# Four merged expert slots per unit, placed irregularly among the score batches of an attention and mixture-of-experts layer

## The reference, cut to what matters

```
q, k, v = xn @ Wq.T, xn @ Wk.T, xn @ Wv.T              # 16 heads of 16
attn    = softmax(q k^T / 16) v                        # 4096 keys and 4096 queries a head
h_e     = silu((xn @ w1_e + b1_e) * (xn @ w3_e + b3_e))    # hidden width 352
experts = shared expert + the two best of 8 experts, weighted by softmax(xn @ gate.T)
```

## Time and profile before

| what | us |
|---|---|
| median of three runs | 2263.67 (2261.61 to 2264.11) |
| the profiled execution, its own time | 2250.58 |
| span of the profiled execution | 2248.8 |
| TensorE busy | 2207.4 (98%) |
| TensorE weight loads | 962.0 (43%) |
| ScalarE busy | 2025.7 (90%) |
| VectorE busy | 793.5 (35%) |
| GpSimd busy | 238.6 (11%) |
| mean granted TensorE clock | 0.996 |

### The profile page before, as it was taken

One profiled execution on the slowest core, in us unless ns is written; L12 is line 12 of the kernel. 1 busy time (PEld: TensorE's weight loads), 2 busy tenths in 40 slices (PEclk: granted clock), 3 DMA queues, 4 the chain that ended last, 5 costly groups with the idle time before them and its releaser, 6 DMA issues.

```text
span 2248.8 us, 38025 instructions
## 1 busy us (share of the span) xinstructions
PE 2207.4 (98%) x15618; PEld 962.0 (43%) x15618; DVE 793.5 (35%) x1514; ACT 2025.7 (90%) x2209; POOL 238.6 (11%) x242
## 2 busy tenths in 40 slices
PE   7989999999999999999999999999999999999998
PEld 3622344444444444444444444444444444444322
DVE  6312133333333333343333333333343333333132
ACT  4579999999999999999999999999999999999997
POOL 1000242223221000000000000000000000000172
PEclk9989999999999999999999999999999999999999
DMA  6661333132232223213132222213213222221142
GB/s 228 214 247 59 81 99 91 59 100 85 75 90 71 64 50 77 74 52 83 41 79 68 73 62 67 74 48 81 73 48 82 62 60 68 79 62 40 49 136 79
DMA packets 219374, 187.28 MB, mean 83 GB/s; under 512 B 107815, under 2 KB 190334, under 8 KB 218942
## 3 DMA queue, kind: packets, MB, share of 16 engines
q1 hardware_dynamic: 207374, 149.41, 23.7%
q0 software_dynamic: 11824, 35.40, 4.8%
HBM read 130.21 MB, written 54.53 MB: 82 GB/s over the span
## 4 chain that ended last, share of the span: by engine, by line
PE 93%; ACT 6%; issue 1%; DVE 0%; DMA 0%; DVEq 0%
PE PS L627 40%; PE PS L614 29%; PE PS L639 13%; PE PS L650 6%; ACT probs L800 6%; PE PS L522 3%; PE PS L559 1%; PE PS L511 0%; PE PS L532 0%; DMA resid<-in_x 0%; DVE ln_t L907 0%; DVE o_t L1093 0%; DVE stats L902 0%; DVE probs L926 0%; ACT hid L791 0%
## 5 line engine op out<-in xcount | busy, mean ns | idle before, releaser
L800 ACT ACTIVATE probs<-PS 128x1024 f32<-128x1024 f32 x2048 | 1935.7, 1083 | 147.7 <-PE PS L614 139.9
L627 PE MATMUL PS<-probs,v_head 128*32 128x512 f32 x8192 | 999.1, 600 | 1.2 <-ACT probs L800 0.8
L614 PE MATMUL PS<-q_ring,k_stack 50*128 50x512 f32 x4096 | 779.0, 454 | 15.5 <-issue 9.7
L614 PEld LDWEIGHTS PS<-q_ring,k_stack 50*128 50x128 f32 x4096 | 319.4, 185 | 599.5 <-ACT probs L800 525.9
L627 PEld LDWEIGHTS PS<-probs,v_head 128*32 128x32 f32 x8192 | 207.2, 109 | 458.9 <-issue 455.5
L1124 DVE SCALAR_TENSOR_TENSOR prod<-PS,bias_sb,gate_in 128x256 f32<-128x256 f32 x165 | 79.6, 482 | 514.7 <-PE PS L639 514.7
L639 PE MATMUL PS<-x_hi,w_hi 128*128 128x256 f32 (+1 forms) x660 | 217.6, 330 | 0.0
L639 PE MATMUL PS<-x_lo,w_hi 128*128 128x256 f32 (+1 forms) x660 | 185.6, 281 | 0.0
L639 PE MATMUL PS<-x_hi,w_lo 128*128 128x256 f32 (+1 forms) x660 | 185.4, 281 | 0.0
L1118 DVE TENSOR_SCALAR gate_in<-PS,bias_sb 128x256 f32<-128x256 f32 x165 | 79.7, 483 | 297.3 <-PE PS L639 297.3
L854 POOL DMA_DIRECT2D slot_y<-y_sb x39 | 27.9, 716 | 1387.3 <-DVE y_sb L1187 1387.3
(11 more groups left out here) (128 smaller groups left out, 1042.2 us busy)
## 6 DMA issues: line engine op xcount, KB each, us to landing
w_raw<-in_w SPq DMA_DIRECT2D x110, 352.0 KB
k_stack<-qk_parts SPq DMA_DIRECT2D x120, 128.0 KB
w_raw<-in_w SPq DMA_DIRECT2D x55, 256.0 KB
q_ring<-qk_parts SPq DMA_DIRECT2D x384, 32.0 KB
slot_x<-part_a SPq DMA_DIRECT2D x39, 256.0 KB, 2.3
slot_in<-slot_x SPq DMA_DIRECT2D x156, 64.0 KB, 2.4
slot_y<-y_sb POOLq DMA_DIRECT2D x39, 256.0 KB, 2.5
k_stack<-qk_parts SPq DMA_DIRECT2D x136, 64.0 KB
```

The source lines that it names most:

```text
L614: last = pe.matmul(bank(2 * score_buffer(turn, g) + r), k_stack[rows, kt * P:(kt + 1) * P], q_ring[rows, sweep, i * QC:(i + 1) * QC], star ...
L627: last = pe.matmul(bank(O_BANK)[VW * j:VW * (j + 1), :], v_head[:, kt, :], probs[:, slot, (j % 2) * QC:(j % 2 + 1) * QC], start=(kt == 0), ...
L800: nc.scalar.activation(probs[:, prob_slot(g), :], bank(2 * score_buffer(h, g), 2), ACT.Exp, scale=ENERGY_SCALE).then_inc(s_exp, 1)
```

## The change

TensorE gets another order within a unit, and three places on the other engines follow it. The eight slots become four: `up_both(u, j)` issues both halves of an up pair without a wait between them (twelve matmuls), and the two `down` calls of a unit stand directly behind each other (18 matmuls). One semaphore count for a pair replaces the two counts (`s_ab`: 3 a unit instead of 6). The score groups come in batches of two or three, the value tiles always in pairs. The number of score groups, value tiles and expert matmuls is the same. Waits for `s_exp` are now made from a running count: a value tile waits by itself where no score group before it has waited for as much.

```
-                last.then_inc(s_ab, 1)
+                return last
...
+            def up_both(u, j):
+                if u >= UNITS:
+                    return
+                if j == 0 and u == 0:
+                    pe.wait_ge(s_prc, 1)
+                if j == 0 and u > 0:
+                    pe.wait_ge(s_prod, 3 * u)
+                if j == 0:
                     pe.wait_ge(s_w13, u + 1)
                     pe.wait_ge(s_xboth, u + 1)
-                    up(u, 0, 0)
-                if i == 1 and u < UNITS:
-                    pe.wait_ge(s_gin, 3 * u + 1)
-                    up(u, 0, 1)
...
+                if j == 1 or (j == 2 and u == 0):
+                    pe.wait_ge(s_prod, 3 * u + j)
+                if j == 2 and u > 0:
+                    pe.wait_ge(s_yc, u)
+                up(u, j, 0)
+                up(u, j, 1).then_inc(s_ab, 1)
+
+            def down_tile(u, t):
+                if u < 0:
+                    return
+                if t == 0:
+                    if u + 1 < UNITS:
+                        pe.wait_ge(s_prod, 3 * u + 5)
+                    pe.wait_ge(s_w2, u + 1)
+                    pe.wait_ge(s_hlo, u + 1)
+                down(u, t)
+
+            issued = [0, 0, 0]
+
+            def next_scores(count):
+                for n in range(issued[0], issued[0] + count):
+                    if n >= SB:
+                        pe.wait_ge(s_exp, n - SB + 1)
+                        issued[2] = max(issued[2], n - SB + 1)
+                    if n < H * GH:
+                        scores(n // GH, n // GH, n % GH)
+                issued[0] += count
+
+            def next_values(count):
+                for m in range(issued[1], issued[1] + count):
+                    if issued[2] < 2 * m + 2:
+                        pe.wait_ge(s_exp, 2 * m + 2)
+                        issued[2] = 2 * m + 2
+                    values(m // GS, m // NT % 2, m % NT)
+                issued[1] += count
...
             def mixed_head(h):
...
+                for u in range((h - 1) * PER_HEAD, h * PER_HEAD):
+                    next_scores(3)
+                    up_both(u, 0)
+                    next_scores(2)
+                    next_values(2)
+                    next_scores(3)
+                    next_values(2)
+                    next_scores(3)
+                    next_values(2)
+                    next_scores(2)
+                    up_both(u, 1)
+                    next_scores(3)
+                    next_values(2)
+                    next_scores(3)
+                    next_values(2)
+                    next_scores(3)
+                    down_tile(u - 1, 0)
+                    down_tile(u - 1, 1)
+                    next_scores(3)
+                    next_values(2)
+                    next_scores(3)
+                    next_values(2)
+                    next_scores(2)
+                    up_both(u, 2)
+                    next_scores(2)
+                    next_values(2)
...
             def gate(u, j):
-                dve.wait_ge(s_ab, 6 * u + 2 * j + 1)
+                dve.wait_ge(s_ab, 3 * u + j + 1)
...
             def product(u, j):
                 dve.wait_ge(s_gin, 3 * u + j + 1)
-                dve.wait_ge(s_ab, 6 * u + 2 * j + 2)
...
             def tokens_hi(u):
-                dve.wait_ge(s_ab, 6 * u)
+                dve.wait_ge(s_ab, 3 * u)
...
                     if u:
                         hidden(u - 1)
-                    if real:
-                        gate(u, 1)
-                    if u:
                         hidden_hi(u - 1)
                         hidden_lo(u - 1)
                     if real:
+                        gate(u, 1)
                         product(u, 1)
```

More of the change, by code:

```diff
@@ L53 @@
 PER_HEAD = 4
-UNIT_STEPS = GS // PER_HEAD
+UNIT_GROUPS = GH // PER_HEAD
 TANH_LAG = 3
@@ L703, in plain_head @@
+            def plain_head(h):
                 for k in range(1, GS + 1):
-                    step_scores(h, k, last)
-                    if first and k == 20:
+                    next_scores(2)
+                    if h == 0 and k == 20:
                         pe.wait_ge(s_mask, 1)
@@ L710, in plain_head @@
                         pe.matmul(bank(F_BANK)[:, NT * E:2 * NT * E], ones_sb[:, :], cm, start=True, stop=True).then_inc(s_pre, 1)
-                    values(h, (k - 1) // NT, (k - 1) % NT)
+                    next_values(1)
             def mixed_head(h):
[L715 to L727, removed]
+                for u in range((h - 1) * PER_HEAD, h * PER_HEAD):
[22 more added lines that the diff above has]
+                    up_both(u, 2)
+                    next_scores(2)
+                    next_values(2)
+            next_scores(SB)
+            plain_head(0)
             for h in range(1, H - 1):
                 mixed_head(h)
-            plain_head(H - 1, last=True)
+            plain_head(H - 1)
         @block.scalar
@@ L802, in _ @@
                     done = (h - 1) * GH + g - TANH_LAG
-                    if done > 0 and done % (2 * UNIT_STEPS) == 0 and done // (2 * UNIT_STEPS) <= UNITS:
-                        tanh(done // (2 * UNIT_STEPS) - 1)
+                    if done > 0 and done % UNIT_GROUPS == 0 and done // UNIT_GROUPS <= UNITS:
+                        tanh(done // UNIT_GROUPS - 1)
         @block.gpsimd
```

## The result

The changed kernel takes 2243.47 us (median of four runs, 2241.7 to 2246.07) against 2263.84 us. The ratio is 0.9913 with a 95% interval of 0.9896 to 0.993: 0.9% faster. The forecast was 2239.7 us. The profiled execution took 2246.07 us, its span is 2244.3 us.

What follows compares the result with a forecast made beforehand. TensorE was taken to bound heads 1 to 14. Merged slots (0.76 us) and score batches (0.80) less added waits gained 0.43 us a unit; 54 units plus 1 us took 2263.67 to 2239.7 us, range 2222 to 2262.

Steps and rivals of the forecast that it cites:

- The unit: One period of TensorE's expert-stage order in heads 1 to 14: from 33.49 to 33.06 us, a gain of 0.43 us.
- the join: Between a merged slot's halves: matmuls follow at 0.12 us without edges, saving 0.76 us a unit over four merges.
- three late third scores: Last group of a second batch of three, three times a unit: 0.14 us wait plus 0.10 penalty, 0.72 us together.
- one wait at group 4: Score group behind the first up pair waits for an exponential behind the tanh: 0.42 us, 0.52 with penalty.
- The waits of the value tiles: Second tiles behind groups 10 and 18 have 0.4 us margin, costing nothing; waits ahead of pairs would cost 0.5 us each.
- plain heads at 117 us: Sign of a right forecast: the first and last heads, whose issue order is unchanged, stay at 117 us.
- rival D: Score waits shorter or without penalty: 2218 us without penalties, 2178 us without any waits; chance 0.10.
- The penalty: A score that has waited costs 0.43 us until the next piece instead of 0.33, so 0.10 us beyond its wait.
- A: The join in merged slots saves nothing: TensorE pays both edges, unit 33.63 us, time 2271 us; chance 0.07.
- B: Scores wait longer for exponentials: each extra 0.1 us adds 0.4 us a unit; at 0.2 us, 2284 us; chance 0.09.
- C: ScalarE is the bound, so nothing moves: 2263.67 us; chance 0.04.
- E: A VectorE order or transfer slips and TensorE waits once a unit: 2264 us or more; chance 0.04.

Runs made afterwards that it cites:

- e2_ahead: Changed kernel with each value-tile pair waiting for both tiles' exponentials ahead of its first tile; 2299.08 us against 2264.85 for the kernel before, ratio 1.0147.
- e5_before_again: The kernel before, unedited, measured and profiled once more; 2265.81 us, with a last head of 129.4 us.
- e7_ends: Changed kernel with units 0 and 55 in a regular order of score batches of two; 2242.41 us against 2266.1 for the kernel before, ratio 0.9891.
- e6_nogather: Changed kernel without the 64 indirect gathers in the last head, zeros added instead; 2233.03 us against 2266.1 for the kernel before, ratio 0.9853.
- e8_split: Changed kernel with one score group between the halves of each merged expert slot; 2292.23 us against 2266.1 for the kernel before, ratio 1.011.
- e4_order: Changed kernel with another paper-derived unit order and the tanh behind group 9's exponential; 2192.71 us against 2264.85 for the kernel before, ratio 0.9676.
- e11_after_again: The changed kernel, unedited, measured once more; 2240.59 us against 2262.24 for the kernel before, ratio 0.99.
- e3_tanh7: Changed kernel with ScalarE's tanh four exponentials later; 2229.69 us against 2264.85 for the kernel before, ratio 0.9843.
- e10_order3: Changed kernel with e4_order's unit order but the tanh in its old place; 2210.57 us against 2250.78 for the kernel before, ratio 0.9823.
- e9_both: e4_order's kernel with units 0 and 55 in the regular order of batches of two; 2177.48 us against 2250.78 for the kernel before, ratio 0.9674.

## Why the prediction was right

*The unit.* Forecast 33.06 us, measured 33.05. ScalarE's wait for scores went down as forecast, but by 34 us (128.5 to 94.3) and not by about 24. The terms hold one by one: the up pair 1.61 (1.63), the down pair 2.35 (2.35), the join 0.12 us, batches of three 0.89 to 0.91 (0.89), three late third scores with a batch of 1.12 to 1.14 (0.24 us more each), and one wait at group 4. That one is 0.73 - 0.34 = 0.39 us and 0.10 of penalty (0.42 and 0.10).

*The waits of the value tiles.* None in the middle of the run, and e2_ahead shows the margin that the prediction counted on.

*The sum.* 54 units times 0.44 us are 24 us. The medians differ by 20.4 us, in the repeat by 21.7. The two executions with pauses, the changed kernel's and e5_before_again's, can be compared stretch by stretch. From the start of unit 0 to the end of unit 55 it is 2104.34 - 248.85 = 1855.5 us against 2123.30 - 248.20 = 1875.1, a gain of 19.6. The steady units give 23.8. Against this stand unit 0, 34.53 against 32.99 us (1.5 lost), unit 55, 33.62 against 32.79 (0.8 lost), and the pauses in units 2 to 12, 2.7 against 1.0 us (1.6 lost).

*What was mis-sized.* Two terms of the sum. Unit 0 was taken as unchanged and unit 55 as 1 us shorter; they were 1.5 and 0.8 us longer, 3.3 us more than forecast for the two. That is the clock: each unit has one value pair at half clock, 3.56 and 3.57 us instead of 1.92, together 3.3 us. Where a slot is missing, its two batches become one of four to six, TensorE waits for each further score, and the clock fell behind these waits (but not in every run, see e7_ends). In e6_nogather, where it didn't in unit 55, that unit took 31.97 us, 0.8 us less than before, as forecast within 0.2 us. The pauses were not in the profile that I read. I carried the 13 us between that execution and the median over as an unexplained constant. That was right for the time, but by luck of its nature: it is a loss in the last head, which the change doesn't touch. For the same reason one sign of being right, plain heads at 117 us, failed in the last head (128.6 us). A slip in rival D is without effect on the forecast: its 31.93 us without any wait still contain the old wait of 0.11 us that the sum takes off, so it should be 31.82 us and about 2172 us.

*The penalty.* The 0.10 us that a waiting score group costs beyond its wait came as forecast. But the single group of e8_split takes the same 0.43 us with no wait, and a value pair in e2_ahead pays nothing extra for its wait. So it is the price of a score group that stands alone rather than of a wait.

*The rivals.* A (the join has an edge) fell to the timeline. B (later scores) fell: no wait is 0.1 us longer than forecast. C (ScalarE is the bound) was wrong by the unit's length, though ScalarE's share of the chain grew. D and E had nothing. The Trainium skill, in Perfetto Trace Analysis, section Identifying the Most-Contended Engine, judges TensorE by its share of peak and its weight load share, and by the second (43%) ScalarE (90%) would have been named. A shorter order on TensorE gave 0.9% all the same, and e4_order 3.2%.

## What to carry to other kernels

Price an order of matmuls by its edges: read what the first and the last matmul of a kind cost beyond the ones between, count the changes of kind, and then walk through one period with the buffers' waits in hand. The place of one odd instruction on the engine that feeds back (here a tanh of 0.73 us on ScalarE) can be worth as much as the whole change (0.44 us a unit): 0.26 by moving it alone, 0.51 in the better order. And before a difference between a profiled execution and the median is carried over, look where it sits.

## What the runs showed of the hardware

A score group that stands alone takes 0.43 us until the next piece starts, two in a batch take 0.66. It is alone when it really waits for its exponential (1049.47 to 1049.90 in the changed kernel) or when it stands between two expert halves without a wait (e8_split). A value pair behind a real wait takes its usual 1.85 us (e2_ahead). A wait that is already met costs nothing that can be seen: the first matmul of a down slot with three waits takes 0.22 us in the kernel before (1001.42 to 1001.64), that of the slot without any also 0.22.

TensorE's granted clock went to half (the 1.2 GHz level) in unit 0 of the changed kernel after a stretch with three waits of 0.65, 0.41 and 0.42 us, and the value pair behind it took 3.56 us instead of 1.92. The same stretch was followed by the half clock in four runs (the changed kernel, e11_after_again, e3_tanh7, e6_nogather) and not in three (e2_ahead, e4_order, e10_order3). What decides between the two is open.

While indirect gathers run, completions of TensorE's scores can come late. In the last head of the changed kernel this happens five times, and ScalarE stands idle for 0.9 to 2.3 us each time; with the half clock that follows some of them, the head is 13 us longer. Without the gathers (e6_nogather) there is none. In one of the four sessions of the experiments the two kernels profiled (e9_both, e10_order3) had none with the gathers in place. What makes them appear is open: no run here separates the gathers' bytes, their descriptors and the instruction supply of TensorE.
